# Turning LayerNorm outputs through a DRAM scratch and 32x32 blocks on VectorE, in a cross-attention and FFN kernel

## What is computed

```
x1 = layernorm(_layernorm(x), ln1_g, ln1_b)        # x: (16, 256, 512)
x2 = layernorm(ctx_768, ln2_g, ln2_b)              # ctx: (16, 256, 384)
q = x1 @ Wq + bq;  k = x2 @ Wk + bk;  v = x2 @ Wv + bv
attn = softmax(einsum('bqe,bke->bqk', q, k) * scaling)
x = x + (attn @ v) @ Wo + bo
h = bitlinear(_layernorm(x), w_fc) + gate * (_layernorm(x) @ v.T @ fast_b.T @ u.T)
r = maximum(h, 0)
out = x + bitlinear(r * r, w_proj)                 # 512 -> 2048 -> 512, ternary weights times a scale
```

## Time and profile before

| | |
|---|---|
| median of 3 runs | 826.78 us (825.85 to 826.89) |
| span of the profiled execution | 823.8 us; some 3.0 us less than the median of the runs |
| granted TensorE clock | 1.000 |
| busy share of the span | PE 98%, PEld 82%, DVE 62%, ACT 45%, POOL 19% |
| DMA | 17485 packets, 36.74 MB, mean 45 GB/s |
| matmuls | 4185 |

### The profile page before, as it was taken

One profiled execution on the slowest core, in us unless ns is written; L12 is line 12 of the kernel. 1 busy time (PEld: TensorE's weight loads), 2 busy tenths in 40 slices (PEclk: granted clock), 3 DMA queues, 4 the chain that ended last, 5 costly groups with the idle time before them and its releaser, 6 DMA issues.

```text
span 823.8 us, 11141 instructions
## 1 busy us (share of the span) xinstructions
PE 809.6 (98%) x4185; PEld 676.0 (82%) x4185; DVE 513.4 (62%) x1052; ACT 374.4 (45%) x712; POOL 154.9 (19%) x175
## 2 busy tenths in 40 slices
PE   6999999999999999999999999999999999999998
PEld 4678788888888888888888888888888888888886
DVE  5998863676447753676537764576536764477434
ACT  5987463425543263424534264424634255432432
POOL 3250320025001230024101150023300250012001
PEclk9999999999999999999999999999999999999999
DMA  9752010101101010101101011101101010000001
GB/s 318 255 148 92 1 52 1 39 1 52 52 3 37 25 45 34 39 1 51 52 1 40 1 52 51 39 1 52 52 1 39 0 52 1 1 2 25 26 1 51
DMA packets 17485, 36.74 MB, mean 45 GB/s; under 512 B 4596, under 2 KB 4998, under 8 KB 17432
## 3 DMA queue, kind: packets, MB, share of 16 engines
q1 hardware_dynamic: 16868, 34.98, 12.3%
q10 hardware_dynamic: 564, 1.06, 0.3%
HBM read 27.64 MB, written 8.39 MB: 44 GB/s over the span
## 4 chain that ended last, share of the span: by engine, by line
PE 94%; DVE 2%; DMA 1%; SPq 1%; issue 0%; ACT 0%; DVEq 0%
PE H L1221 28%; PE O L1201 28%; PE G L1091 24%; PE G L1119 4%; PE H L1227 4%; DMA Wv_s<-in_L_xattn_Wv_dram 1%; PE H L1075 1%; PE H L1119 1%; PE G L1167 1%; PE O L1275 1%; PE H L1091 1%; PE H L1068 1%; PE O L1242 1%; SPq L460 0%; PE O L1246 0%
## 5 line engine op out<-in xcount | busy, mean ns | idle before, releaser
L1221 PE MATMUL H<-xnT,fcT 128*128 128x512 f32 x1024 | 257.3, 393 | 0.0
L1201 PE MATMUL O<-projT,qbuf 128*128 128x512 f32 x992 | 249.0, 393 | 0.0
L1221 PEld LDWEIGHTS H<-xnT,fcT 128*128 128x128 f32 x1024 | 188.3, 188 | 36.8
L1201 PEld LDWEIGHTS O<-projT,qbuf 128*128 128x128 f32 x992 | 183.2, 188 | 36.8 <-DVE qbuf L986 0.3
L717 ACT ACTIVATE qbuf<-rbuf 128x512 fp32r<-128x512 f32 x125 | 79.0, 632 | 124.1 <-PE O L1201 62.4
L986 DVE TENSOR_TENSOR qbuf<-rbuf,qbuf 128x512 fp32r<-128x512 f32 x125 | 93.2, 745 | 64.1 <-ACT qbuf L717 64.1
L982 DVE TENSOR_TENSOR rbuf<-rbuf 128x512 f32<-128x512 f32 x128 | 98.7, 771 | 50.8 <-ACT rbuf L709 49.7
L709 ACT ACTIVATE rbuf<-H,scf 128x512 f32<-128x512 f32 x128 | 87.5, 683 | 80.3 <-PE H L1227 80.2
L570 POOL TENSOR_TENSOR xrs<-xrs,mhalf 128x4 f32<-128x4 f32 x9 | 9.5, 1050 | 347.0 <-DVE xrs L966 347.0
L1091 PE MATMUL G<-n1T,M 128*128 128x512 f32 x276 | 64.2, 390 | 0.0
L1091 PE MATMUL G<-Wvo,tT 128*128 128x512 f32 x270 | 64.2, 390 | 0.0
(11 more groups left out here) (169 smaller groups left out, 996.8 us busy)
## 6 DMA issues: line engine op xcount, KB each, us to landing
xb<-in_x_dram SPq DMA_DIRECT2D x8, 1024.0 KB
ctxb<-in_ctx_dram SPq DMA_DIRECT2D x8, 768.0 KB
wring<-in_L_ffn_w_fc_dram SPq DMA_DIRECT2D x16, 256.0 KB, 5.5
wring<-in_L_ffn_w_proj_dram SPq DMA_DIRECT2D x16, 256.0 KB, 3.8
out_dram<-x2a SPq DMA_DIRECT2D x8, 512.0 KB, 2.6
out_dram<-x2b SPq DMA_DIRECT2D x6, 512.0 KB, 2.6
Wq_s<-in_L_xattn_Wq_dram SPq DMA_DIRECT2D x4, 256.0 KB, 4.0
x2a<-in_L_xattn_Wo_dram ACTq DMA_DIRECT2D x1, 1024.0 KB, 9.3
```

The costliest lines, as they stand in the source:

```text
L1201: mm = pe.matmul(banks[f"O{t}"][:, :], qbuf[:, j % 2, h, t * P:(t + 1) * P], projT[:, j, :], start=(j == 0 and h == HI), stop=(j == NFF - ...
L1221: pe.matmul(banks[f"H{j % 2}"][:, :], fcT[:, k, j * P:(j + 1) * P], xnT[:, h, k, :], start=(k == 0 and h == HI), stop=False)
```

## The change

The turns by TensorE of n1, n2 and x are kept for group 0 alone, in the prologue. For groups 1 to 7 the rows (fp32, in n1_rows, ctxb and x_rows) take another way:

- SyncE writes them to a DRAM scratch with four transfers, one for each quadrant of 32 partitions, and waits for these.
- SyncE reads them back with four transfers, each into one quadrant of partitions, in pieces of 32 fp32 elements (128 B): 8192 pieces for n1 and x each, 6144 for n2. Now the 32x32 blocks lie where their turned form belongs.
- VectorE turns the blocks, in steps "n1raw k", "n2raw k", "xraw k" of 128x512 (4, 3 and 4 a body). ScalarE copies the high part ("n1hi", "n2hi", "xhi"), VectorE subtracts for the low part ("n1lo", "n2lo", "xlo"), both from and to SBUF.

BODY_TABLE becomes BODY_ORDER, a written order for each engine. The norms of n1 and n2 for a body are made at the end of the one before ("nx0+", "nc0+"). The buffers are laid over others so that all fits: raw data lie under the finished halves, and even and odd groups have a buffer each. The core of the diff:

```diff
+BODY_ORDER = {
+    "pe": (
+        "down-:14 L:0 down-:15 up:0 up:1 up:2 down:0 up:3 down:1 up:4 down:2 up:5 t:0 t:1 t:2 down:3 s:0 up:6 s:1 s:2 "
+        "down:4 pT:0 up:7 s:3 down:5 pT:1 up:8 down:6 w:0 w:1 up:9 w:2 down:7 a:0 a:1 up:10 a:2 down:8 a:3 up:11 "
+        "down:9 up:12 down:10 up:13 down:11 up:14 down:12 up:15 down:13 "
+    ).split(),
+    "act": (
+        "L:0 up:0 hi:0 up:1 hi:1 n1hi0 up:2 n1hi1 hi:2 n1hi2 up:3 n1hi3 hi:3 up:4 n2hi0 n2hi1 t:0 n2hi2 hi:4 t:1 up:5 "
+        "t:2 hi:5 s:0 n2:0 up:6 s:1 n2:1 s:2 n2:2 pT:0 n2:3 s:3 hi:6 pT:1 up:7 hi:7 up:8 w:0 hi:8 w:1 w:2 up:9 hi:9 "
+        "up:10 hi:10 up:11 hi:11 nx0+ nx1+ up:12 hi:12 up:13 nx2+ hi:13 nx3+ nc0+ xhi0 up:14 nc1+ xhi1 hi:14 xhi2 "
+        "up:15 nc2+ xhi3 hi:15 nc3+ "
+    ).split(),
+    "dve": (
+        "L:0 out01 out23 n1raw0 sq:0 lo:0 n1raw1 sq:1 lo:1 n1raw2 sq:2 n1lo0 lo:2 n1lo1 n1raw3 n1lo2 sq:3 n1lo3 lo:3 "
+        "n2raw0 n2raw1 n2lo0 t:0 n2raw2 sq:4 n2lo1 n2lo2 lo:4 t:1 t:2 sq:5 s:0 n2:0 s:1 lo:5 n2:1 s:2 sq:6 n2:2 pT:0 "
+        "n2:3 s:3 xs01+ lo:6 sq:7 pT:1 lo:7 sq:8 w:0 w:1 xs23+ w:2 lo:8 a:0 a:1 sq:9 nX0 lo:9 sq:10 nX1 a:2 lo:10 a:3 "
+        "nX2 sq:11 nX3 lo:11 cs01+ sq:12 cs23+ lo:12 sq:13 xraw0 xraw1 lo:13 xraw2 sq:14 xlo0 xraw3 lo:14 xlo1 xlo2 "
+        "sq:15 xlo3 lo:15 "
+    ).split(),
...
-        "B.x:0 B.x:1 B.x:2 B.x:3 B.L:0 sprow_out B.up:0 B.hi:0 B.up:1 store:30 store:31 B.hi:1 "
+        "x:0 x:1 x:2 x:3 nx0+ nx1+ nx2+ nx3+ B.L:0 sprow_out B.up:0 B.hi:0 B.up:1 store:30 store:31 B.hi:1 nc0+ nc1+ nc2+ nc3+ "
...
+            def move_blocks(g, blocks, rows, written, moved, scratch):
+
+                sp.wait_ge(moved, MOVES * (g - 1))
+                for i in range(4):
+                    sp.dma_start(scratch[:, i, :], rows[32 * i:32 * i + 32, :, :].rearrange("p t d -> p (t d)")
+                                 ).then_inc(written, 16)
+                sp.wait_ge(written, 64 * g)
+                for q in range(4):
+                    sp.dma_start(blocks[32 * q:32 * q + 32, :, :, :, :].rearrange("p i t k n -> p (i t k) n"),
+                                 scratch.rearrange("p i (m n) -> p (i m) n", n=P)[:, :, 32 * q:32 * q + 32]
+                                 ).then_inc(moved, 16)
...
+            def move_n1(g):
+
+                sp.wait_ge(n1_made, 4 * (g + 1))
+                sp.wait_ge(unit_full, n_full(g - 2, ("a", 3)))
+                move_blocks(g, n1_blocks, n1_rows, n1_written, n1_moved, n1_scratch)
+
+            move_n1(1)
+            for b in range(NG - 1):
+                g = b + 1
+                sp.wait_ge(n2_made, 4 * (g + 1))
+                sp.wait_ge(n1_moved, MOVES * g)
+                move_blocks(g, n2_blocks, ctxb, n2_written, n2_moved, n2_scratch)
+                if b > 0:
+                    store(b - 1, (b - 1) % 2)
+                if b + 2 < NG:
+                    load_x(b)
+                    load_ctx(b)
+                sp.wait_ge(xn_made, 4 * (g + 1))
+                sp.wait_ge(unit_full, n_full(b, ("s", 3)))
+                move_blocks(g, x_blocks, x_rows, x_written, x_moved, x_scratch)
+                if b + 2 < NG:
+                    move_n1(b + 2)
...
+                    elif kind[:4] == "xraw":
+                        k = int(kind[4])
+                        dve.wait_ge(x_moved, MOVES * (b + 1))
+                        nc.vector.transpose(raw_of[(b + 1) % 2][:, LO, k, :],
+                                            x_blocks[:, :, :, k, :].rearrange("p i t n -> p t i n")
+                                            ).then_inc(xraw_made, 1)
+                    elif kind[:3] == "xlo":
+                        k = int(kind[3])
+                        raw, halves = raw_of[(b + 1) % 2], group_of[(b + 1) % 2]
+                        dve.wait_ge(xhi_made, KD * b + k + 1)
+                        nc.vector.tensor_tensor(halves[:, LO, k, :], raw[:, LO, k, :], halves[:, HI, k, :],
+                                                ALU.subtract).then_inc(xlo_made, 1)
```

More of the change, by code:

```diff
@@ L60, in units_before @@
         return 0
[L61 removed]
+    return b * sum(map(kept, BODY)) + sum(map(kept, FIRST))
 def count(b, unit, kept=lambda u: True):
@@ L111, in bank_before, with step, body_steps @@
             return b - 1, u
-BODY_TABLE = [
[11 rows of a table removed]
-]
-def placed(engine, h):
-    column = {"pe": 1, "act": 2, "dve": 3, "pool": 3}[engine]
-    return [row[0] for row in BODY_TABLE if row[column] == h]
-def body_steps(attention, leftover, engine):
-    out = ["nX2", ("x", 0), "nX3", ("x", 1)] if engine == "dve" else [("x", 0), ("x", 1)]
-    if leftover:
-        out += [("down-", NFF - 2)]
-    out += [("x", 2), ("x", 3)]
-    if leftover:
-        out += [("down-", NFF - 1), "out01"]
-    else:
-        out += ["xs01", "xs23", "cs01", "cs23"]
-    out += [("L", 0)]
-    if leftover:
-        out += ["out23"]
-    for j in range(NFF if attention else FIRST_LATE):
-        out += [("up", j)]
-        out += placed(engine, 2 * j) if attention else []
-        out += [("sq", j), ("hi", j)]
+BODY_ORDER = {
[4 rows of a table added]
+    ).split(),
+    "act": (
[4 rows of a table added]
+    ).split(),
+    "dve": (
[5 rows of a table added]
+    ).split(),
+    "pool": (
+        "out23 residual xs23+ a:0 a:1 a:2 a:3 cs23+ "
+    ).split(),
+}
+def step(word):
+    kind, _, n = word.partition(":")
+    return (kind, int(n)) if n else kind
+def body_steps(b, engine):
+    if b < GROUPS - 1:
+        skipped = [word for word in BODY_ORDER[engine] if word[-1] == "+" and b == GROUPS - 2
+                   or word.startswith(("down-", "out")) and b == 0]
+        return [step(word) for word in BODY_ORDER[engine] if word not in skipped]
+    out = [("down-", NFF - 2), ("L", 0), ("down-", NFF - 1), "out01", "out23"]
+    for j in range(FIRST_LATE):
+        out += [("up", j), ("sq", j), ("hi", j)]
         if j >= 2:
             out += [("down", j - 2)]
-        out += placed(engine, 2 * j + 1) if attention else []
         out += [("lo", j)]
-    if not attention:
-        for j in (NFF - 3, NFF - 2):
-            out += [("up", j), ("sq", j), ("hi", j), ("lo", j)]
-        out += [("up", NFF - 1), ("down", NFF - 5), ("sq", NFF - 1), ("hi", NFF - 1), ("lo", NFF - 1)]
+    for j in (NFF - 3, NFF - 2):
+        out += [("up", j), ("sq", j), ("hi", j), ("lo", j)]
+    out += [("up", NFF - 1), ("down", NFF - 5), ("sq", NFF - 1), ("hi", NFF - 1), ("lo", NFF - 1)]
     return out
@@ L219, in prologue_steps @@
         else:
-            steps.append((b, (kind, int(n)) if n else kind))
+            steps.append((b, step(word.removeprefix("B."))))
     return steps
@@ L304, in mk_xattn_ffn @@
         xb = sb("xb", [P, TILES, D])
+        with ExitStack() as below_both:
+            x_rows = sb("x_rows", [P, TILES, D], F32, below_both)
         pbuf = sb("pbuf", [P, TILES, S])
@@ L417, in run_bodies @@
                 steps(b, [st])
-            steps(0, [st for st in body_steps(True, False, engine) if (0, st) not in early])
-            for b in range(1, NG - 1):
-                steps(b, body_steps(True, True, engine))
-            steps(NG - 1, body_steps(False, True, engine))
+            steps(0, [st for st in body_steps(0, engine) if (0, st) not in early])
+            for b in range(1, NG):
+                steps(b, body_steps(b, engine))
         block = stack.enter_context(nc.Block())
@@ L1104, in unit @@
                     job_read(pe, max(n for n in range(len(JOBS)) if f"H{n % 2}" == name))
-                elif un in (("x", 2), ("x", 3)) and not (b == 0):
-                    pe.wait_ge(relu_made, NFF * (b - 1) + NFF - 1 + (t == 3))
                 elif before:
@@ L1116, in unit @@
                                  "n2T": (ctxb[:, t, :], n2_made)}[kind]
-                    pe.wait_ge(made, 4 * (b if kind == "x" else b + 1) + t + 1)
+                    pe.wait_ge(made, 4 * (b + 1) + t + 1)
                     for k in range(KC if kind == "n2T" else KD):
```

177 lines of the change are left out of this document (113 added, 64 removed), and 15 rows, old and new, of tables (BODY_TABLE, PROLOGUE).

## The result

The changed kernel takes 847.98 us (median of 4 runs, 846.4 to 850.74) where the kernel before took 826.84 on the same chip (825.85 to 827.31): a ratio of 1.0265, 95% interval 1.0244 to 1.0287. It is slower, by 21 us. The forecast was 820.1, faster, with a range up to 850.

A forecast was written before the change was run, and what follows sets the result against it. TensorE was taken as the bound. From 826.8 us, 36.5 for removed turns came off, 25.2 for waits on x and 4.6 once in body 0 were added: 820.1 us, range 797 to 850.

The forecast's parts named there:

- The turns' worth: TensorE, bodies 0 to 6: 44 turns fewer save 5.21 us a body, 36.5 in seven; a body without waits takes 89.53.
- Rows of x ready: After the last attention projection (a 3) ends on TensorE, x's rows are complete 4.3 us later.
- x's way: From a 3 through scratch to the next body's lo 14: 22.9 us against 19.3 available; TensorE waits 3.6 a body, 25.2 in all.
- the two transfer terms: x's move through DRAM: four writes from 32 partitions take 5.2 us, reading 8192 pieces of 128 B takes 8.0.
- the turning point: No gain remains at a wait of 4.4 us a body, or x's write and read together at 14.2 us.
- half rate from 32 partitions: Rival: transfers from and to 32 partitions run at half rate; write 6.5 us, reads unchanged, total 830.5; chance 0.2.
- small pieces: Rival: pieces dearer than those of u_s; read 3 us longer gives 844, by bytes some 890; chance 0.15.
- The estimate of 10.5: x's read if a 128 B packet costs 7 cycles against 5 for 64 B: 10.5 us, total 840; 8.0 was taken.
- The holes slow TensorE itself: Rival: TensorE's steps after a wait run slower; at most a us or so a body, inside the range; no chance given.
- Once 4.6: Body 0: L's later start costs 0.7 us, n1's late arrival delays up 4 by 3.9; 4.6 in all, one time.
- The place of the wait: TensorE was to wait before down 14, released by lo 14.
- just hidden: n1's blocks arrive 7.2 us into the next body, VectorE stands there from about 8.3; from 9.0 each us costs one; priced at nothing.

The follow-up runs named there:

- e7: Changed kernel with x moved in two halves and n1's rows written first, ahead of x's move; 850.65 us, ratio 1.0295 to the kernel before.
- e10: Changed kernel with x in halves, body 0's n1 steps later, n1's write between x's second write and its read; 821.55 us, ratio 0.9946 to the kernel before.
- e3: Changed kernel with the reads of x's blocks in 8 KB runs in place of 128 B pieces; 820.08 us, ratio 0.9931 to the kernel before.
- e4: Changed kernel with x's rows written by one 1 MB transfer from 128 partitions and strided turns on VectorE; 841.21 us, ratio 1.0185 to the kernel before.
- e2: Changed kernel with 22 unused matmuls filling TensorE's hole ahead of down 13; 846.07 us, ratio 1.0245 to the kernel before.
- e5: Changed kernel with x moved in two halves, the first leaving as soon as its rows are ready; 811.72 us, ratio 0.9827 to the kernel before.
- e1: Changed kernel with x's blocks read early from the input x, so TensorE doesn't depend on the write; 812.67 us, ratio 0.9838 to the kernel before.
- e6: Changed kernel with n1's rows made early and written ahead of x's move; 850.18 us, ratio 1.028 to the kernel before.

## Why the prediction was wrong, by its own steps

**Right.** The turns' worth: the bodies without any wait, body 6 of e7 and of e10, take 89.57 and 89.54, where the sum had 89.53. Rows of x ready 4.0 behind a 3, 4.3 forecast. The place: x's way, with lo 14 as its last link and 6.9 us from the blocks to L, against 5.2 + 1.81 = 7.0. The turn on VectorE 0.70, taken as 0.6; VectorE at 64% is no bound.

**Wrong, the step on which the sign hung: the two transfer terms.** The write was taken as 5.2 and took 6.3; the reads as 8.0 and took 10.3. From write to blocks it is 16.6 instead of 13.4 (16.2 in the mean of the seven bodies). The prediction put the turning point at 14.2 for write and read together. Both rivals that it kept apart came true at once, and each had been priced nearly right: half rate from 32 partitions at + 1.3, small pieces at + 2.5 to 3. Their sums stood at 830.5 and 840 to 844; with both at once and the body shown, 820.1 + 8 x (1.1 + 2.3) = 847.3, seven times for x and once for n1 in body 0, it would be nearly the 848. By the means (0.9 and 2.1) it is 844, and the rest came from elsewhere, as below. e3 and e4 take away one each.

The write from 128 partitions takes 3.9, the lower bound that the prediction worked out from plain stores, and from 32 it takes 6.3. The Trainium skill, "SBUF — State Buffer", section "Door 1: The DMA port swizzle", has the rule that partitions 0 to 31 reach 8 of 16 ports. The traces agree: 213 GB/s a quadrant at a time against 388 from all 128 partitions, and the four quadrants land one after another, so that issuing them together doesn't make up for it.

The reads in 8 KB runs take 6.8 and in 128 B pieces 10.3. The estimate of 10.5 came from the Trainium skill, "DMA: Bandwidth & Descriptors", section "Why small descriptors are slow (HBM only)". The total agrees, but in part by luck: the 8192 packets take 7.8 us where the rule made 8.7 of the 6.2, and what lies ahead of them and behind is 2.3 and not 1.8. In the traces a piece of 64 B costs 0.75 ns (1.6 us for 2132) and one of 128 B 0.95, a factor of 1.27. The prediction's own 8.0 counted the pieces and left their size out, and that is what it had too small.

**Wrong: "The holes slow TensorE itself ... At most a us or so a body".** The steps behind a hole lost 1.6 to 3.0 us. The earlier trace rows had a hole of 3.03 us at full clock, and a hole of 5 was never looked at. What it costs in the end is 0.9 a body (e2), since VectorE's chain covers the rest. So the sentence held as a price, by a cover that it didn't name, and it counts 6 us that the sum left out.

**Wrong in size: "Once 4.6".** Body 0 is 18.3 us over (106.0 for 87.7), of which x's way has 8.3 (L comes 29.2 behind a 3, and 20.9 in e5, without a hole), so 10.0 once. n1's blocks arrive 16.1 behind its rows, 13.4 forecast, for the same two reasons; the wait ahead of up 4 is 6.4 for 3.9; the slow up and a wait ahead of a t add 3.0.

**The place of the wait.** It stands ahead of down 13, not 14: where the blocks are later than forecast, lo 13, behind two turns, is late as well. With the fill of e2 a small wait ahead of down 14 shows. The price is the same, as L ends the chain either way.

**The account.** In the seven bodies the miss is 684.3 - (624.9 + 25.2 + 4.6) = 29.6 us. Bodies 1 to 6 have 3.25 each of it (96.38 for 93.13), 19.5 in all; body 0 has 10.1, 4.7 on x's way and 5.4 on n1's. The 3.25 are, in the mean of the six, transfers + 2.7 and tail + 0.6, the clock's work, less 0.35 as the rows were early; another + 0.2 is that TensorE's work up to L is 20.9 and not 21.1 (19.3 + 1.81). By spans the miss is 848.7 - 817.1 = 31.6, with the 2.0 ahead of the first mark; by medians it is 848.0 - 820.1 = 27.9, since the profiled execution was a slow one of its four. That x's way carries it is shown by e1 and e5: 35 and 36 us faster than the changed kernel with the same turns.

**What came next.** n1's way was "just hidden", limit 9.0. It was hidden by x's lateness alone; as soon as x is in time (e1, e5) it costs 1.5 to 1.7 a body. And the queue is a resource of its own: e7 and e10 moved n1 ahead and lost more on x's way than they won, and in e6 the gain in body 0 was lost in the prologue and in longer bodies.
